# Self-attention: Q and K split into float32r parts on GpSimd, exact transposed scores as one float32r product a head

## The reference

```python
qkv = x @ W_qkv.T + b_qkv
q, k, v = ...  # 8 batches, 16 heads, 128 positions, 8 columns
scores = jnp.einsum('bhqd,bhkd->bhqk', q, k) / math.sqrt(Hd)
bias = -slopes[:, None, None] * rel
probs = jax.nn.softmax(scores + bias[None], axis=-1)
out = jnp.einsum('bhqk,bhkd->bhqd', probs, v)
...
return out @ W_out.T + b_out
```

## Time and profile before

| | us |
|---|---|
| median of 3 runs | 671.83 (669.29 to 679.17) |
| the profiled execution, first to last instruction | 685.9 |
| TensorE busy in it | 633.7 (92%) |
| weight loads | 519.4 (76%) |
| VectorE | 436.2 (64%) |
| ScalarE | 315.9 (46%) |
| GpSimd | 221.7 (32%) |

### The profile page before, as it was taken

How to read it: one execution, slowest core, us unless ns; L and a number is a source line. 1 busy time by engine, 2 the same in 40 slices (tenths; PEclk the granted TensorE clock), 3 DMA queues, 4 the chain that set the end, 5 groups by cost and what they waited for, 6 DMA issues and landing times. The chain is left out here.

```text
span 685.9 us, 12856 instructions
## 1 busy us (share of the span) xinstructions
PE 633.7 (92%) x4884; PEld 519.4 (76%) x4900; DVE 436.2 (64%) x1083; ACT 315.9 (46%) x644; POOL 221.7 (32%) x307
## 2 busy tenths in 40 slices
PE   2978999899998899999899998999998999999998
PEld 2556568788887788889666676888886877888887
DVE  3485365556666755654666754666666667888886
ACT  2595124344434423324544443445554465666653
POOL 7012440146558810002011100343557502333330
PEclk9987599899999999998999997999999899999999
DMA  7602100100000011000000002000011013222011
GB/s 197 149 0 59 46 1 0 48 1 2 1 1 25 24 46 43 6 1 1 2 1 2 2 1 94 2 1 1 3 47 47 1 49 92 77 77 78 31 32 31
DMA packets 24828, 22.69 MB, mean 33 GB/s; under 512 B 5808, under 2 KB 20536, under 8 KB 24768
## 3 DMA queue, kind: packets, MB, share of 16 engines
q1 hardware_dynamic: 24768, 21.88, 11.2%
HBM read 20.92 MB, written 0.56 MB: 31 GB/s over the span
## 5 line engine op out<-in xcount | busy, mean ns | idle before, releaser
L1552 ACT ACTIVATE sb_shared<-bank 128x512 f32<-128x512 f32 (+1 forms) x64 | 36.0, 595 | 73.3 <-PE bank L1420 73.3
L3050 PE MATMUL bank<-sb_ff_xt_high,sb_ff_low 128*128 128x512 f32 x128 | 51.0, 398 | 0.0
L1622 DVE TENSOR_REDUCE sb_ca_m<-bank 128x4 f32<-128x512 f32 (+1 forms) x56 | 35.5, 675 | 24.0 <-PE bank L1394 24.0
L3050 PE MATMUL bank<-sb_ff_xt_high,sb_ff_high 128*128 128x512 f32 x128 | 50.6, 396 | 0.0
L3050 PE MATMUL bank<-sb_ff_xt_low,sb_ff_high 128*128 128x512 f32 x128 | 50.1, 392 | 0.0
L1666 DVE TENSOR_TENSOR sb_ca_o<-bank,sb_ca_rinv 128x384 f32<-128x384 f32 (+1 forms) x90 | 46.1, 513 | 3.1
L1660 DVE RECIPROCAL sb_ca_rinv<-bank 128x3 f32<-128x3 f32 (+1 forms) x90 | 15.5, 172 | 46.4 <-PE bank L1443 40.2
L2782 ACT ACTIVATE sb_ca_kt<-bank 128x512 f32<-128x512 f32 x32 | 19.1, 598 | 56.1 <-PE bank L2693 55.9
L1443 PE MATMUL bank<-sb_c_vo,sb_shared 128*128 128x130 f32 x256 | 37.0, 287 | 4.1 <-DVE sb_ca_o L1666 3.3
L1443 PE MATMUL bank<-sb_ca_vo,sb_shared 124*128 124x130 f32 x256 | 35.5, 280 | 3.7 <-DVE sb_ca_o L1666 3.2
L1443 PEld LDWEIGHTS bank<-sb_ca_vo,sb_shared 124*128 124x128 f32 x256 | 32.3, 190 | 6.9 <-DVE sb_ca_o L1666 5.7
(11 more groups left out here) (466 smaller groups left out, 1721.3 us busy)
## 6 DMA issues: line engine op xcount, KB each, us to landing
sb_ca_vo<-cw_t_dram SPq DMA_DIRECT2D x8, 512.0 KB, 3.8
sb_ff_w<-in_L_ffn_w_dram SPq DMA_DIRECT2D x8, 256.0 KB, 2.7
sb_ff_gate_up<-in_L_ffn_w_gate_dram SPq DMA_DIRECT2D x8, 256.0 KB, 3.0
sb_ff_gate_up<-in_L_ffn_w_up_dram SPq DMA_DIRECT2D x8, 256.0 KB, 3.3
sb_ff_down<-in_L_ffn_w_down_dram SPq DMA_DIRECT2D x8, 256.0 KB, 4.6
sb_ff_w<-in_L_ffn_w_dram SPq DMA_DIRECT2D x8, 128.0 KB, 2.8
sb_x<-in_x_dram SPq DMA_DIRECT2D x1, 512.0 KB, 5.0
sb_c_o<-in_L_xattn_w_out_dram SPq DMA_DIRECT2D x1, 512.0 KB, 7.8
```

The costliest lines, as they stand in the source:

```text
L1552: nc.scalar.activation(pt[0:KS, c, :], score_bank(j, c)[0:KS, :], ACT.Exp).then_inc(exp_done, 1)
L1622: V.tensor_reduce(m[n % 2][:, heads_of(c)], s[:, :, 0:KS], AX, ALU.max, negate=True).then_inc(s_read, 1)
L3050: mm = nc.tensor.matmul(ps[:, :], wp[p][:, g, t * P:(t + 1) * P], xs[xp][:, cols], start=(q == 0), stop=(q == 2))
```

## The change

`wqk` gets the head's 8 columns three times in a strip, so that the projections put the same 8 values on rows 0 to 7, 8 to 15 and 16 to 23; the biases `bqk` are loaded onto all three groups of rows (24 transfers, now issued behind the second cross-attention's weights). `qt` and `kt` become float32r tiles (rounded float32, whose product takes one record in the trace, as in L3050). ScalarE and VectorE copy the projections into float32 tiles `q_all` and `k_all` (two buffers each); then Q's row group 8 to 15 and K's row group 16 to 23 are replaced by their rounding remainder: a multiplication with a 0/1 mask a row (`low_rows`) gives `q_high` or `k_high` as float32r, and `q_all - q_high` (or `k_all - k_high`) is written as float32r. Over the 24 rows one product then sums high x high, low x high and high x low. GpSimd does this for every batch's Q and for K from batch 2 on; VectorE does it for K of batches 0 and 1. `scores` waits for `q_split` and `k_split` in place of the copies. `scores_t` is the same code, on float32r tiles.

```diff
-        qt, kt, v = some(3, "qt", [P, T, P]), some(3, "kt", [P, T, P]), some(3, "v", [P, NH, VW])
+        qt, kt, v = some(3, "qt", [P, T, P], F32R), some(3, "kt", [P, T, P], F32R), some(3, "v", [P, NH, VW])
+        q_all, k_all = some(2, "q_all", [P, T, P]), some(2, "k_all", [P, T, P])
+        q_high, k_high, low_rows = sb("q_high", [P, T, P], F32R), sb("k_high", [P, T, P], F32R), sb("low_rows", [P, 2])
...
+            def split_q(n):
+                pool.wait_ge(q_copied, n + 1)
+                nc.gpsimd.tensor_scalar(q_high[:, :, :], q_all[n % 2][:, :, :], low_rows[:, 0:1], None, ALU.mult).then_inc(q_high_done, 1)
+                pool.wait_ge(q_high_done, n + 1)
+                nc.gpsimd.tensor_tensor(qt[n % 3][:, :, :], q_all[n % 2][:, :, :], q_high[:, :, :], ALU.subtract).then_inc(q_split, 1)
+
+            def split_k(n):
+                pool.wait_ge(k_copied, n + 1)
+                pool.wait_ge(k_split, n)
+                nc.gpsimd.tensor_scalar(k_high[:, :, :], k_all[n % 2][:, :, :], low_rows[:, 1:2], None, ALU.mult).then_inc(k_high_done, 1)
+                pool.wait_ge(k_high_done, n + 1)
+                nc.gpsimd.tensor_tensor(kt[n % 3][:, :, :], k_all[n % 2][:, :, :], k_high[:, :, :], ALU.subtract).then_inc(k_split, 1)
...
             for n in range(3, NB):
                 rstd(n)
+                split_q(n - 1)
+                split_k(n - 1)
                 add_bo(n)
+            split_q(LAST)
+            split_k(LAST)
             steps.gpsimd_steps(pool)
...
                 if c0 == 0:
-                    pe.wait_ge(q_copied, n + 1)
-                    pe.wait_ge(k_copied, n + 1)
+                    pe.wait_ge(q_split, n + 1)
+                    pe.wait_ge(k_split, n + 1)
...
-            nc.scalar.mul(wqk[:, 0, :, 0:W], heads(0), SCALE).then_inc(wt_copied, 1)
-            nc.scalar.copy(wqk[:, 1, :, 0:W], heads(1)).then_inc(wt_copied, 1)
+            thrice = lambda k: wqk[:, k, :, 0:3 * W].rearrange("p h (r w) -> p h r w", r=3)
+            of_heads = lambda k: bc(heads(k).unsqueeze(2), [P, NH, 3, W])
+            nc.scalar.mul(thrice(0), of_heads(0), SCALE).then_inc(wt_copied, 1)
+            nc.scalar.copy(thrice(1), of_heads(1)).then_inc(wt_copied, 1)
...
+            def split_first_k(n):
+                dve.wait_ge(k_copied, n + 1)
+                V.tensor_scalar(k_high[:, :, :], k_all[n][:, :, :], low_rows[:, 1:2], None, ALU.mult).then_inc(k_high_done, 1)
+                dve.wait_ge(k_high_done, n + 1)
+                V.tensor_tensor(kt[n][:, :, :], k_all[n][:, :, :], k_high[:, :, :], ALU.subtract).then_inc(k_split, 1)
```

More of the change, by code:

```diff
@@ L161, in load_later_weights @@
     pg.load(sp, "self", sw["bo"][:, :], a["L1_attn_b_out"].partition_broadcast(P))
+    load_cross1_weights(pg, sp)
+    load_low_rank_weights(pg, sp)
     bqk = a["L1_attn_b_qkv"][0:2 * D].rearrange("(k t c w) -> c w k t", k=2, t=NH // NCH, c=NCH)
@@ L165, in load_later_weights @@
             for k in range(2):
-                pg.load(sp, "self", sw["bqk"][32 * c:32 * c + D // NH, k, :], bqk[c][:, k, :])
-    load_cross1_weights(pg, sp)
-    load_low_rank_weights(pg, sp)
+                for r in range(3):
+                    first = 32 * c + r * (D // NH)
+                    pg.load(sp, "self", sw["bqk"][first:first + D // NH, k, :], bqk[c][:, k, :])
 def setup(pg, fold0):
@@ L2009, in self_attention @@
          st_ready, bias_added, exp_done, av_ready, av_copied, avt_ready, rinv_done, o_done, ot_ready, ot_copied,
-         out_ready, bo_added, x_done) = pg.sems("sa", (
+         out_ready, bo_added, x_done, strips_marked, q_high_done, k_high_done, q_split, k_split) = pg.sems("sa", (
             "wt_ready zeroed wt_copied bias_scaled var_ready rstd_ready norm_order xn_ready xt_ready xt_copied "
@@ L2013, in self_attention @@
             "st_ready bias_added exp_done av_ready av_copied avt_ready rinv_done o_done ot_ready ot_copied "
-            "out_ready bo_added x_done"))
+            "out_ready bo_added x_done strips_marked q_high k_high q_split k_split"))
         sb = lambda n, s, dt=F32: pg.sbuf(f"sa_{n}", s, dt, ctx=ctx, side="right")
@@ L2055, in add_bo @@
                 nc.gpsimd.tensor_tensor(pg.x[:, n, :], pg.x[:, n, :], bo[:, :], ALU.add).then_inc(bo_added, 1)
+            def split_q(n):
[9 more added lines that the diff above has]
+                nc.gpsimd.tensor_tensor(kt[n % 3][:, :, :], k_all[n % 2][:, :, :], k_high[:, :, :], ALU.subtract).then_inc(k_split, 1)
             for n in range(3):
                 rstd(n)
+            pool.wait_ge(strips_marked, 2)
+            split_q(0)
+            split_q(1)
             pg.wait_loads(pool, "self")
@@ L2269, in copy_q @@
                 act.wait_ge(q_ready, n + 1)
+                if n >= 2:
+                    act.wait_ge(q_split, n - 1)
                 for t in range(T):
-                    ins = nc.scalar.activation(qt[n % 3][:, t, :], q_ps[:, t * P:(t + 1) * P], ACT.Identity, bias=bqk[:, 0, t:t + 1])
+                    ins = nc.scalar.activation(q_all[n % 2][:, t, :], q_ps[:, t * P:(t + 1) * P], ACT.Identity, bias=bqk[:, 0, t:t + 1])
                 ins.then_inc(q_copied, 1)
@@ L2367, in copy_k @@
                 dve.wait_ge(k_ready, n + 1)
-                V.tensor_tensor(kt[n % 3][:, :, :], k_ps[:, :].rearrange("p (t k) -> p t k", t=T),
+                if n >= 2:
+                    dve.wait_ge(k_split, n - 1)
+                V.tensor_tensor(k_all[n % 2][:, :, :], k_ps[:, :].rearrange("p (t k) -> p t k", t=T),
                                 bc(bqk[:, 1, :].unsqueeze(2), [P, T, P]), ALU.add).then_inc(k_copied, 1)
+            def split_first_k(n):
[3 more added lines that the diff above has]
+                V.tensor_tensor(kt[n][:, :, :], k_all[n][:, :, :], k_high[:, :, :], ALU.subtract).then_inc(k_split, 1)
             def add_v(n):
@@ L2409, in add_out @@
                 V.tensor_tensor(pg.x[:, j, :], out_ps, pg.x[:, j, :], ALU.add).then_inc(x_done, 1)
+            strips = pg.ident[:, :].rearrange("p (c r) -> p c r", c=NCH)
+            for k in range(2):
+                V.tensor_reduce(low_rows[:, k:k + 1], strips[:, :, W * (k + 1):W * (k + 2)], mybir.AxisListType.XY,
+                                ALU.add).then_inc(strips_marked, 1)
             pg.wait_loads(dve, "self")
@@ L2422, in _ @@
             copy_k(0)
+            dve.wait_ge(strips_marked, 2)
+            split_first_k(0)
             add_v(0)
@@ L2428, in _ @@
             copy_k(1)
+            split_first_k(1)
             add_v(1)
```

## The result

The changed kernel takes 705.8 us (median of 4 runs, 701.0 to 719.2), the kernel before 671.1 beside it: a ratio of 1.0485, 95% interval 1.041 to 1.056, slower. The forecast was slower, 692.0 us; the measured time lies 0.8 us above the end of its range (705). The kernel before ran a little faster here than in the forecast's median; by the ratio, 1.0485 times that median of 671.83 us, the changed kernel would stand at 704.4, just inside the range.

What follows compares the result with a forecast made beforehand. The prediction took TensorE's own stream to bound the self-attention loop, with GpSimd nearly free. Turns 8.4, start 3.0, end -1.3 made 10.1 us, and lowered clock 10 more: from 671.8 to 692 us, range 678 to 705.

Steps and rivals of the forecast that it cites:

- Exact scores: In each `scores_t` call, float32r halves the 16 records: 0.45 us off a call, bounds 0 and 0.76.
- Rival 4: In `scores_t`, a float32r product of 128 columns costs as much as now: 699 us; chance 0.06.
- The split on GpSimd: Per operand on GpSimd: mask 1.70 us, subtraction 1.30, handovers 0.15, together 3.15; Q's hides, K's doesn't.
- Rival 3: In the loop, K's split is cheap and scores much cheaper, so not slower: 668 us; chance 0.06.
- The chain: Scores to K's projection, copy, split, next scores: 11.72 us a turn against 10.32; six turns cost 8.4 us more.
- The start: First batches' splits, VectorE's held up beside GpSimd's: 3.0 us more at the stage's start, bounds 1.85 and 4.5.
- The end: Four `scores_t` calls after the last split save 1.8 us, less waits for ScalarE's exponentials: 1.3 us less.
- rival 2: In the turns, the VectorE-GpSimd port delays K's copy: 0.75 us a turn, 4.5 in all, 697 us; chance 0.10.
- The clock: TensorE's seven new stops each bring 3 us of low clock, costing 1.4 each: 10 us, bounds 0 and 19.
- warm sum: Self-attention stage without the clock term: 8.4 + 3.0 - 1.3 = 10.1 us more.

Runs made afterwards that it cites:

- filled run: Changed kernel with the split waits behind the two identity products opening the scores, each issued four times: 681.6 us, ratio 1.0127 to the kernel before.
- e5_masks_act: Changed kernel with both masks made on ScalarE instead of GpSimd, subtractions left on GpSimd: 695.5 us, ratio 1.0269 to the kernel before.
- e6_early_k: Changed kernel with K projected and copied about 3 us earlier in the turn, whole split on GpSimd: 700.2 us, ratio 1.0325 to the kernel before.

## Why the prediction was right, and by how much it fell short

- **Exact scores: right.** 0.45 us off a call forecast, 0.50 measured (the forecast's own rule, half of 16 records that take 1.00 us from start to start, gives 0.50 too; its 0.45 has no row), and both calls lie on the path (turn 9.35 without the split). Rival 4 fell.
- **The split on GpSimd: right.** Mask 1.70 forecast, 1.56 measured; subtract 1.30, measured 1.26; copy's end to split's end 3.15, measured 3.00. Rival 3 fell with it.
- **The chain: right.** 11.72 us a turn forecast. The filled run's turn at full clock is 11.34 and hides the pair of products, 0.53 (345.86 to 346.39 in the trace after): 11.87. Six turns cost 9.3 us, forecast 8.4.
- **The start: right in the sum, with the port one batch later.** From the first transpose to the loop 21.80 us after (298.69 to 320.49), 17.57 in the second profile of before (297.68 to 315.25): 4.2 more. Two projections took 1.95 and 1.91 us there at half clock instead of 1.16 and 1.06, which is 1.6; 2.6 are left for the chain, forecast 3.0. The forecast had VectorE's split of the first batch's K held up beside GpSimd; that subtraction took 0.69 us (at 307.10), and the second batch's was held, 1.63 us, as the earlier trace rows suggested. VectorE's maxima come behind it, and their transpose waits 0.93 us for VectorE:

```profile
314.82 1.31 POOL L2065 TENSOR_TENSOR sb_sa_qt<-sb_sa_q_all,sb_sa_q_high 128x512 fp32r<-128x512 f32 x1
315.05 1.63 DVE L2405 TENSOR_TENSOR sb_sa_kt<-sb_sa_k_all,sb_sa_k_high 128x512 fp32r<-128x512 f32 x1
318.63 0.23 PE L2148 MATMUL bank<-sb_ident_bf,sb_sa_nm 128*128 128x128 bf16 x1 [0.93 <-DVE sb_sa_nm L2424]
```

- **The end: right.** 1.3 less forecast; where the clock held (the run with the waits moved) it was 13.20 - 12.23 = 1.0 less.
- **The port in the turns (rival 2): there, but off the path.** In the change as made, VectorE's subtraction of the maxima is held once for a whole instruction of GpSimd:

```profile
367.04 1.27 POOL L2065 TENSOR_TENSOR sb_sa_qt<-sb_sa_q_all,sb_sa_q_high 128x512 fp32r<-128x512 f32 x1
367.05 1.33 DVE L2424 TENSOR_TENSOR sb_sa_nm<-sb_sa_m,sb_sa_nm 128x64 bf16<-128x64 f32 x1
...
369.41 0.22 PE L2148 MATMUL bank<-sb_ident_bf,sb_sa_nm 128*128 128x128 bf16 x1
```

The transpose of the maxima starts at 369.41 behind TensorE's own work, without a wait. The rule of the Trainium skill (SBUF — State Buffer, section "SBUF: two separate sides"), that the later one waits for the whole of the earlier, agrees with 1.33 beside 1.27.

- **The clock: the step that failed.** The forecast took "the middle, 3 us" of low clock for each of seven stops, 21 us, 10 us of time, and bounded it by 6 us each, 19 us of time. Measured were 58 us, beyond that bound. The price of a microsecond was about right: 34 us in all less the chain's 9.3 + 2.6 - 1.0 = 10.9 leaves 23 for 58 us, 0.40 each (forecast 0.46). What was wrong is the one short length for every stop. Behind the first six stops the low stretches stayed apart, about 3 to 9 us each and 32 us together (forecast 18), and the turns came out at 13.4 to 15.8 us (forecast 12 to 13.5). Behind the seventh, of 2.96 us at 403.53, TensorE worked without a pause and the clock stayed at 0.50 until 426.2, well past the last split: 23 us (forecast 3). The rest of the 58 lies inside the stops. The third stop's stretch, the fifth's, and the last with the end of the stop ahead of it:

```profile
345.86:351.60 5.74, 5.74 (x44) 4.30 (x45) 2.86 (x7) 1.96 (x5) 0.84 (x2) 0.70 0.00 0
372.89:381.90 9.01, 9.01 (x60) 5.71 (x60) 3.90 (x9) 2.37 (x6) 2.23 (x3) 0.51 0.01 2
402.30:426.20 23.90, 22.67 (x171) 15.32 (x172) 8.36 (x18) 7.05 (x15) 5.29 (x6) 0.50 0.01 1
```

Why the last stretch lasted so long stays open. The row that the length was taken from was an exception, too: in the first profile of before a stop of 1.48 us is followed by 6 us at 0.50; the same stop leaves the clock at 1.00 in the twelve other profiles, for example in the second one of before:

```profile
297.68 0.63 PE L2184 MATMUL bank<-sb_ident,sb_sa_w_nat 128*128 128x128 f32 x4 [1.49 <-PEq L1195]
```

```profile
300.00:306.00 6.00, 6.00 (x61) 5.67 (x61) 2.28 (x8) 2.96 (x8) 2.34 (x6) 1.00 0.00 0
```

So the warm sum (the change's cost at full clock), 10.1 forecast and 10.9 measured, was the smaller part of the loss, and the clock, put at half of 20, was two thirds of 34. That the forecast of 706 for a profiled execution came close to the measured span of 702.5 was luck: before's first profiled execution, on which it was built, was itself 18.4 us longer than its second (685.9 and 667.5), with a lower clock in stages that the change doesn't touch.

## What to carry to other kernels

Where TensorE bounds a stage at full clock, a wait that opens once a turn is to be priced twice: the length of the stop, and the clock of the turns behind it, which here was twice the first. The second price can't be read off the length of a stop: stops of 1.74 us were followed by either clock in one run (`e5_masks_act`), and in another (`e6_early_k`) two of 0.66 and 0.51 us by the low one. An operand's preparation that is moved to an idle engine is hidden only if it starts early enough in the turn and doesn't share a port with what the path waits for; check both in the timeline before counting the engine as free. When such a stop can't be avoided, put products that are due anyway into it (waits behind them): half a microsecond of them in each stop was worth 12 here.

## What the runs showed that I had not expected

- Products whose results are overwritten made the kernel faster: from a ratio of 1.0309 with the waits moved to 1.0127 with these products as well.
- The same kernel has 20.5 us at half clock in one execution and none there in another: the block of the kernel before began at 309.05 and at 297.68 us. The rows of 64.8 to 85.3 us in its two profiles:

```profile
64.80:85.30 20.50, 19.11 (x49) 10.66 (x51) 6.84 (x16) 5.34 (x11) 10.80 (x20) 0.50 0.31 86
```

```profile
64.80:85.30 20.50, 19.09 (x85) 10.20 (x86) 14.19 (x31) 7.20 (x16) 16.84 (x27) 1.00 0.31 85
```

TensorE is equally busy in both, 19.1 us, and does 49 instructions in the one and 85 in the other. A busy share alone doesn't tell work done.
- Shorter turns at 1.00 came with one turn at 0.74 that before hadn't: what four turns gained, 0.7 us each, was given back in one.
